# Gate logits folded into the scores and sums products of a pre-norm MoE decoder layer, with routing one period later

## What is computed

```python
# linear attention, 8 heads of 64, elu(.) + 1 as the feature map of q and k
x = x + linear_attention(LN(x))
# cross attention to 77 context rows; scores are normalised per row, then softmax
q = LN(x) @ xWq + xbq; k = ctx @ xWk + xbk; v = ctx @ xWv + xbv
s = q @ k.T / sqrt(512); s = (s - mean(s)) / (std(s, ddof=1) + 1e-8) + mask * -1e-32
x = x + tile(softmax(s) @ v, 16) @ Wout + bout
# mixture of 8 experts, top 2, capacity 1280 rows each, first come first served
h = LN(x); logits = h @ Wg.T; top_v, top_i = top_k(logits, 2); gates = softmax(top_v)
pos = cumsum(one_hot(top_i)) - 1; keep = pos < 1280
x = x + sum over kept choices of gate * ((gelu(h @ W1a) * (h @ W1b)) @ W2)[expert]
```

## Time and profile before

| | |
|---|---|
| runs of the kernel | 1607.64, 1612.87, 1614.09 us; median 1612.87 |
| the profiled execution | 1614.39 us; its span 1612.7 us |
| mean granted clock of TensorE in it | 0.958 of full speed |
| busy: TensorE, VectorE, ScalarE, POOL | 1507.6, 662.7, 542.6, 360.3 us |
| second stage, from 289.6 to 554.0 us | 264.4 us, TensorE busy 236.72, granted clock 0.86 |
| from 554.0 to 591.0 us | 37.0 us, TensorE busy 4.40 |

### The profile page before, as it was taken

The page is one execution under the profiler, slowest core; times in us unless marked ns, Lnnn a source line. Parts: engine busy times, 40 slices in busy tenths (PEclk is TensorE's granted clock), DMA queues, the critical chain, the costliest instruction groups (busy, mean ns, idle before and its releaser), DMA issues.

```text
span 1612.7 us, 21589 instructions
## 1 busy us (share of the span) xinstructions
PE 1507.6 (93%) x7686; PEld 1271.4 (79%) x7687; DVE 662.7 (41%) x1393; ACT 542.6 (34%) x881; POOL 360.3 (22%) x354
## 2 busy tenths in 40 slices
PE   6999999899998549999999989999999999999998
PEld 5778877788876338788888968888978978898886
DVE  6635555576777614331143243114532332214311
ACT  5334333244433414331143243124432332124311
POOL 3213123135543520201211220121121121021011
PEclk9999999998998569999999999999999999999999
DMA  9101222044424431521233252123452162024122
GB/s 190 53 1 52 80 79 105 1 157 132 99 85 131 131 105 54 157 60 31 37 121 91 52 145 70 33 33 117 124 159 46 36 175 46 20 52 130 22 43 26
DMA packets 78987, 132.23 MB, mean 82 GB/s; under 512 B 30388, under 2 KB 30516, under 8 KB 77912
## 3 DMA queue, kind: packets, MB, share of 16 engines
q1 hardware_dynamic: 62520, 97.40, 20.6%
q0 software_dynamic: 16416, 34.16, 11.4%
HBM read 93.63 MB, written 37.91 MB: 82 GB/s over the span
## 4 chain that ended last, share of the span: by engine, by line
PE 82%; DVE 5%; issue 3%; DMA 3%; POOL 3%; ACT 2%; another core or an unknown queue 1%; SPq 0%; ACTq 0%; POOLq 0%; DVEq 0%
PE pg L877 15%; PE pg L878 15%; PE pg L879 15%; PE pj L877 9%; PE pj L879 8%; PE pj L878 8%; PE pj L1079 2%; POOL slot_table L574 2%; PE pg L1048 1%; PE pg L1128 1%; PE pt L1226 1%; DMA stage<-w 1%; DVE w_lo L1289 1%; PE pt L1070 1%
## 5 line engine op out<-in xcount | busy, mean ns | idle before, releaser
L877 PE MATMUL pg<-xe_hi,w_hi 128*128 128x512 f32 (+2 forms) x1088 | 393.9, 362 | 22.4 <-issue 10.6
L878 PE MATMUL pg<-xe_lo,w_hi 128*128 128x512 f32 (+2 forms) x1088 | 393.1, 361 | 0.0
L879 PE MATMUL pg<-xe_hi,w_lo 128*128 128x512 f32 (+2 forms) x1088 | 392.6, 361 | 0.0
L1641 DVE TENSOR_TENSOR hp<-gl,pg 128x512 f32<-128x512 f32 (+1 forms) x136 | 87.1, 641 | 606.1 <-ACT gl L830 596.1
L632 POOL DMA_INDIRECT out_rows<-ost,etab x62 | 100.3, 1618 | 800.0 <-ACT ost L857 396.3
L877 PEld LDWEIGHTS pg<-xe_hi,w_hi 128*128 128x128 f32 x1088 | 207.6, 191 | 54.2 <-issue 12.2
L879 PEld LDWEIGHTS pg<-xe_hi,w_lo 128*128 128x128 f32 x1088 | 207.7, 191 | 28.3
L830 ACT ACTIVATE gl<-pg 128x512 f32<-128x512 f32 (+1 forms) x136 | 76.1, 560 | 457.0 <-PE pg L879 452.7
L878 PEld LDWEIGHTS pg<-xe_lo,w_hi 128*128 128x128 f32 x1088 | 207.5, 191 | 28.3
L877 PE MATMUL pj<-w_hi,hg_hi 128*128 128x512 f32 x464 | 183.4, 395 | 0.0
L879 PE MATMUL pj<-w_hi,hg_lo 128*128 128x512 f32 x464 | 180.8, 390 | 0.0
(11 more groups left out here) (220 smaller groups left out, 2067.6 us busy)
## 6 DMA issues: line engine op xcount, KB each, us to landing
stage<-w SPq DMA_DIRECT2D x96, 512.0 KB, 5.2
xr<-x SPq DMA_DIRECT2D x8, 1024.0 KB, 7.6
out_rows<-xr SPq DMA_DIRECT2D x8, 1024.0 KB, 4.7
x_rows<-xn SPq DMA_DIRECT2D x8, 1024.0 KB
x_in<-x SPq DMA_DIRECT2D x7, 1024.0 KB, 5.2
late_xT<-xT_hi SPq DMA_DIRECT2D x2, 1024.0 KB, 3.9
late_xT<-xT_lo SPq DMA_DIRECT2D x2, 1024.0 KB, 6.0
xT_hi<-late_xT SPq DMA_DIRECT2D x2, 1024.0 KB, 6.1
```

The costliest lines, as they stand in the source:

```text
L877: nc.tensor.matmul(o, lh, rh, start=start, stop=False)
L878: nc.tensor.matmul(o, lh, rl, start=False, stop=False)
L879: return nc.tensor.matmul(o, ll, rh, start=False, stop=stop)
L1641: v.tensor_tensor(hp[j % 2][:, 0:w], gl[j % 2][:, 0:w], pg[:, 2 + j % 2, 0:w], ALU.mult).then_inc(s_hp, 1)
```

## The change

The logits are linear in x2 = x1 + values / sum, so they are split: the x1 part comes with the scores (eight more columns of the 96 in `wqk`, filled with `wgp`), the value part with the sums (`slg`: `emask` and vp times wgp, nine columns instead of one). VectorE adds the two (`logits`). x2 is not turned any more; `xT3`, `turn_and_route` and `logits_out` go. New in the first stage, at `s == 2`: `turn_vp` and `value_logits` on TensorE, `vp_turned_out` and `value_logits_out` on VectorE. Routing stands last in VectorE's period, and positions, slots and `dest` follow in the next. The late jobs move one place. ScalarE's `normalise3` moves from the start of a period to behind `gate_exp`. In the last period POOL's scatter of group 6 is cut in two around `norm3(7)`.

```diff
-LATE_AT = {(-1, 0): [0], (0, 0): [1], (0, 1): [2], (0, 2): [3], (1, 0): [4], (1, 1): [5], (1, 2): [6],
+LATE_AT = {(-1, 0): [0], (-1, 2): [1], (0, 0): [2], (0, 1): [3], (0, 2): [4], (1, 0): [5], (1, 1): [6],
...
@@ SP
-                    if g == 2 * q:
+                    if g == q:
@@ POOL
-                    scatter(g - 2)
-                late_q(late(g, 0))
-                late_q(late(g, 1))
+                    scatter(g - 2, range(TI * TOPK))
+                late_q(late(g - 1, 2))
                 if g + 1 < GROUPS:
                     rstd_1(g + 1)
                 else:
-                    scatter(g - 1)
+                    scatter(g - 1, range(TI * TOPK // 2))
+                late_q(late(g, 0))
                 norm3(g)
                 if g + 1 < GROUPS:
                     sigma(g + 1)
-                late_q(late(g, 2))
+                else:
+                    scatter(g - 1, range(TI * TOPK // 2, TI * TOPK))
+                late_q(late(g, 1))
@@ ScalarE
             for g in range(GROUPS):
-                if g >= 1:
-                    normalise3(g - 1)
...
                 turned(sT[:], 0)
-                late_q(late(g, 0))
+                late_q(late(g - 1, 2))
                 if g >= 1:
                     gate_exp(g - 1)
-                late_q(late(g, 1))
+                    normalise3(g - 1)
                 if g + 1 < GROUPS:
-                    turned_rows(xT2, range(TI), 1)
-                    late_q(late(g, 2))
...
-                turned_rows(xT3, range(TI), 1)
-                if g + 1 < GROUPS:
+                    turned_rows(xT2, range(2), 1)
+                    late_q(late(g, 0))
+                    late_q(late(g, 1))
+                    turned_rows(xT2, range(2, TI), 1)
...
                     score_exp(g + 1)
@@ TensorE
+            def turn_vp():
+
+                pe.wait_ge(s_vpev, 1)
+                for b in range(NB):
+                    for m in range(KC):
+                        ins = nc.tensor.transpose(pt[b][:, m * CK:(m + 1) * CK],
+                                                  vp[:, b * D + m * P:b * D + (m + 1) * P], ident[0:CK, 0:CK])
+                ins.then_inc(s_xset, 1)
+
+            def value_logits():
+
+                pe.wait_ge(s_xev, 3)
+                for b in range(NB):
+                    for m in range(KC):
+                        ins = mm(pt[0][0:CK, b * EX:(b + 1) * EX], vpT[:, b, m * CK:(m + 1) * CK], wgp[:, m, :],
+                                 start=m == 0, stop=m == KC - 1)
...
+            def scores(g, at):
+                if g:
+                    pe.wait_ge(s_sinv, g)
+                if g >= 2:
+                    pe.wait_ge(s_posev, g - 1)
...
-                    ins = mm(pj[0][:, i:i + 1], sT[:, i * P:(i + 1) * P], emask[:, b:b + 1], start=True, stop=True)
+                    ins = mm(pj[0][:, SUMS + i * (1 + EX):SUMS + (i + 1) * (1 + EX)], sT[:, i * P:(i + 1) * P], slg[:, b, :],
+                             start=True, stop=True)
...
-            late_q(late(-1, 0), -1)
             attend(0, range(2))
             keys_values(1)
             attend(0, range(2, TI))
+            late_q(late(-1, 0))
...
+            at_x1 = turn_x1(0, range(TI))
+            scores(0, at_x1)
+            attend(1, range(2))
+            late_q(late(-1, 2))
             for g in range(GROUPS):
                 more_groups = g + 1 < GROUPS
-                if more_groups:
-                    attend(g + 1, range(2))
                 at_e = turn_exp(g)
-                late_q(late(g, 0), g)
-                if g:
-                    positions(g - 1)
                 if more_groups:
                     attend(g + 1, range(2, TI))
-                late_q(late(g, 1), g)
+                if g >= 1:
+                    positions(g - 1)
+                sums(g, at_e)
+                late_q(late(g, 0))
                 if more_groups:
-                    at_x1 = turn_x1(g + 1, range(2), 1)
-                values(g, at_e)
+                    at_x1 = turn_x1(g + 1, range(2))
+                    late_q(late(g, 1))
+                values(g, range(2))
                 if more_groups:
...
+                    at_x1.update(turn_x1(g + 1, range(2, TI)))
+                values(g, range(2, TI))
+                if more_groups:
+                    scores(g + 1, at_x1)
+                    if g + 2 < GROUPS:
+                        attend(g + 2, range(2))
+                    late_q(late(g, 2))
+                else:
+                    positions(g)
@@ VectorE
+                ins = v.tensor_copy(lgx[g % 2][:], pj[0][:, 0:TI * PADW].rearrange("p (i c) -> p i c", c=PADW)
+                                    [:, :, CK:CK + EX])
...
+            def logits(g):
+
+                dve.wait_ge(s_sum, g + 1)
+                both = pj[0][:, SUMS:SUMS + TI * (1 + EX)].rearrange("p (i c) -> p i c", c=1 + EX)
+                v.reciprocal(sinv[:], both[:, :, 0])
+                v.tensor_copy(lgs[:], both[:, :, 1:1 + EX]).then_inc(s_sinv, 1)
+                dve.wait_ge(s_sinv, g + 1)
+                link(v.tensor_tensor(lgs[:], lgs[:], sinv[:].unsqueeze(2).broadcast_to([P, TI, EX]), ALU.mult))
+                v.tensor_tensor(lg[:], lgs[:], lgx[g % 2][:], ALU.add).then_inc(s_lg, 1)
...
             def positions_out(g):
 
                 dve.wait_ge(s_pos, g + 1)
+                if g + 1 < GROUPS:
+                    dve.wait_ge(s_sum, g + 2)
...
             for g in range(GROUPS):
-                if g >= 1:
-                    logits_out(g - 1)
-                    route(g - 1)
...
+                logits(g)
+                if not more_groups:
+                    route(g)
                 cross_out(g)
-                if 1 <= g < GROUPS - 1:
-                    gates(g - 1)
-                    place_tokens(g - 1)
-                if g + 1 < GROUPS:
+                if more_groups:
                     score_stats(g + 1)
+                    if g >= 1:
+                        place_tokens(g - 1)
                     softmax(g + 1)
+                    route(g)
+                gate_diff(g)
```

More of the change, by code:

```diff
@@ L126, in decoder @@
     sinv = keep("sinv", [P, TI])
+    slg = keep("slg", [CK, NB, 1 + EX])
+    lgx = [keep(f"lgx{q}", [P, TI, EX]) for q in range(2)]
+    lgs = keep("lgs", [P, TI, EX])
     lg = keep("lg", [P, TI, EX])
@@ L569, in norm3, with scatter @@
                 p.tensor_tensor(shift[1][:], neg_mean[1][:], rstd[1][:], ALU.mult).then_inc(s_rstd3, 1)
-            def scatter(g):
+            def scatter(g, columns):
                 pool.wait_ge(s_dest, g + 1)
-                for c in range(TI * TOPK):
+                for c in columns:
                     p.indirect_dma_start(
@@ L774, in _ @@
             late_q(late(-1, 0))
[L775 removed]
+            turned_rows(xT2, range(TI), 1)
             def score_exp(g):
@@ L889, in turn @@
                         pe.wait_ge(s_vpev, 1)
+                    if s == 3:
+                        pe.wait_ge(s_xev, 4)
                     if s == NG + 1:
@@ L952, in project @@
                         xattn_values()
+                    if s == 2 and j == TI:
+                        turn_vp()
+                    if s == 2 and j == TI + 1:
+                        value_logits()
                     if s or j >= 2:
@@ L1061, in bank, with turn_x1 @@
                 return pt[k]
[L1063 removed]
+            def turn_x1(g, tiles):
                 at = {}
                 for i in tiles:
[L1066 to L1068 removed]
+                    pe.wait_ge(s_x1, g * TI + i + 1)
+                    to = bank((1 + i) % 2)
                     for k in range(KC):
[L1070 removed]
+                        ins = nc.tensor.transpose(to[:, k * P:(k + 1) * P], xr[g % 4][:, i, k * P:(k + 1) * P],
+                                                  ident[:])
                     ins.then_inc(s_bt, 1)
@@ L1114, in turn_exp, with sums, values @@
                 return nt[0]
-            def values(g, at):
+            def sums(g, at):
                 b = g // NG
                 pe.wait_ge(s_btev, at)
-                if g:
-                    pe.wait_ge(s_posev, g)
                 for i in range(TI):
-                    ins = mm(pj[0][:, i:i + 1], sT[:, i * P:(i + 1) * P], emask[:, b:b + 1], start=True, stop=True)
+                    ins = mm(pj[0][:, SUMS + i * (1 + EX):SUMS + (i + 1) * (1 + EX)], sT[:, i * P:(i + 1) * P], slg[:, b, :],
+                             start=True, stop=True)
                 ins.then_inc(s_sum, 1)
-                for i in range(TI):
+            def values(g, tiles):
+                b = g // NG
+                for i in tiles:
                     if g + 1 < GROUPS and i % 2 == 0:
@@ L1378, in xattn_scores_out, with vp_turned_out, value_logits_out @@
                                   src.rearrange("p (b c) -> p b c", b=NB))
+                for b in range(NB):
+                    v.tensor_copy(wqk[:, :, b * PADW + CK:b * PADW + CK + EX], wgp[:])
```

(17 more changed lines are left out.)

142 lines of the change are left out of this document (48 added, 94 removed).

## The result

| | before | after |
|---|---|---|
| runs of the kernel, us | 1607.64, 1612.87, 1614.09, 1612.79 | 1665.28, 1664.80, 1660.50, 1662.37 |
| median, us | 1612.83 | 1663.59 |
| ratio, 95% interval | | 1.0316 (1.029 to 1.034) |
| span of the profiled execution | 1612.7 | 1663.6 |

The changed kernel is slower by 3.2%, outside the range (1588 to 1628). The stretches of its profile, against those of the earlier trace rows: us, busy PE, PEld, DVE, ACT, POOL, PEclk, DMA share, GB/s. The first seven are the periods between score exponentials, then come the tail to the end of the last scatter, the way to the first expert product, and the expert stage.

The account below looks back on a forecast made before the run. TensorE bounds the periods before; afterwards a chain through TensorE and VectorE. Periods +1.6, tail -3.2, first stage +2.7, opening +0.8 sum to +1.9; with the shown median 1.5 lower than the profiled execution, 1615 us, range 1588 to 1628.

Parts of the forecast that it names:

- Expert stage: The final stage, 1022.13 us of the profile: claimed to be left alone by the change, so 0.
- slower rival: Low clock outlasts the first projection and takes values, turn and scores too: +12 us, 1627; chance 0.25.
- Added work in the first stage: 8 transposes (0.9) and 8 small products (1.8) on TensorE, VectorE's copies hidden beside a projection: +2.7 us.
- The tail: Eighth exponential to last scatter: earlier routing and a split scatter shorten POOL's chain from 45.5 to 42.3 us, -3.2.
- The periods: Seven periods between score exponentials: 186.5 us at full clock plus 30 for clock falls, 216.5 against 214.87, +1.6.
- the walk: Step-by-step timing of one new period: 28.4 us at full clock, bound by a chain through TensorE and VectorE.
- new wait for frl: In a period, TensorE's second projection waits for ScalarE's late copies and reads of the first projection's bank: 1.8 us.
- The clock: TensorE's granted clock falls to half in every period, losing 5 us in each of six: 30 us.
- full-clock rival: TensorE's clock holds in the periods: 1585 us without any fall, 1600 taken with half of them; chance 0.29.
- Late results: Scatter beside a 1 MB store makes ScalarE and VectorE see TensorE's results late; moving normalise3 counted as no gain.

Follow-up runs that it names:

- a_pad32: Changed kernel plus 32 one-element activations on ScalarE ahead of its expert loop: 1630.62 us, ratio 1.0116 to the kernel before.
- p_front: a_pad32 with value_logits one projection later on TensorE and VectorE: 1624.12 us, ratio 1.0059 to the kernel before.
- a_pad20: Changed kernel plus 20 one-element activations on ScalarE ahead of its expert loop: 1630.45 us, ratio 1.0129 to the kernel before.
- a_pad128: Changed kernel plus 128 one-element activations on ScalarE ahead of its expert loop: 1661.95 us, ratio 1.0290 to the kernel before.
- p_fill: a_pad32 plus unused 96-column filler products at the end of TensorE's periods (28 or 60 each): 1648.09 us, ratio 1.0224 to the kernel before.
- v_store: p_front plus two dest and pack buffers, second projection behind values 0 and 1, and normalise3 ending ScalarE's periods except the last: 1608.10 us, ratio 0.9972.
- c_pair: p_front plus two dest and pack buffers, and attention_out's second pair ahead of positions_out on VectorE: 1606.34 us, ratio 0.9954 to the kernel before.

## Why the prediction was wrong

**Expert stage, 0, measured +30.1: the step that decided it.** I wrote that the change "leaves alone" that stage, and took instructions to be free of place. Removing ScalarE's copies of x2 moved its loop, and each of seven jumps back then cost 7.8 to 9.8 us, against 1.0 to 1.9 before. Without that effect the change is +17 us (a_pad32, ratio 1.0116), 2.6 us above the top of the range, and of the sign of the slower rival.

**Added work in the first stage, +2.7, measured +8.7.** 1.6 us of it were there before the second transposes (16.52 against 14.95 us, weights that arrived later; the runs differ by as much). The failed step is "VectorE's six small copies and the wait for s_xev lie beside a projection": the projection was too short a cover, the wait 2.67 us, and the clock fell behind it for 3.4 us, which at half rate loses 1.7. The added products themselves took 0.50 and 1.13 us (1.6, 2.7 forecast). These make 7.6 of the 8.7 us; 1.1 were not traced. p_front takes out 6.5 us of the kernel's time; in its trace the way from the second transposes to the `k_sum` products is 270.45 us, against 276.11 in the changed kernel and 268.99 before.

**The tail, -3.2, measured +3.3.** I counted the landing of each scatter only as POOL's own wait, and took norm3(7) to stand ready. I did not ask what is queued behind VectorE's dest(6). By terms: first scatter 10.7 (9.9 forecast), wait 6.4 (5.6), norm3 late by 3.5 (0), last wait 5.1 (3.5), which is 6.7 of the 6.5 us missed, the halves being slightly shorter.

**The periods, 216.5, measured 222.3: nearly right.** With the same instructions in the periods a_pad20 and a_pad128 took 217.7, nearer still, but the 5 us between them come from which falls an execution gets, and that the walk did not foresee. Periods 2 to 5 sum to 134.2 us against 4 x 33.4 = 133.6. The walk's new wait for frl was 1.9 us in each of five (1.8 forecast), VectorE waits for values as said. TensorE's busy time was 24.5 to 29.4 us (26 to 28 forecast). The walk's 28.4 at full clock is 29.4 where a trace shows it, in a period without a scatter. Two errors lie in it: positions_out was taken as free at t = 6.4, and it ended a wait at 10.8 to 10.9 in every period with a scatter, and the sixth period took 32.8 us, not 28.7, since that late second pair held values for 3.8 us and the clock was at 0.70. In the walk itself 0.3 us of the 28.4 has no term: softmax ends at 28.1.

**The clock.** "I expect a fall in every period" held for six of the seven. Periods 2 to 5 are 4.1 us over the 29.43 on the mean (5 forecast), so the size was fair; the full-clock rival failed. The rule of the Trainium skill by which it would have come (TensorE: Matmul & The Clock Gate, HAM oscillation) explains falls by idle gaps; p_fill, with no gap over 1.3 us for some 10 us ahead of a fall, does not agree with that as the whole cause. What does hold the clock was not settled.

**The slower rival** (the low clock taking in values and scores) is what the sixth period shows, at some 4 us, and not the 12 that I gave it (half of the 2 x 7.9 and 12 that it names would be 14); the result had its sign for other reasons.

**Late results.** "Where the scatter's descriptors and a 1 MB store run together" names the wrong partner: v_store has no such store beside the scatter, and VectorE's wait is the same. The forecast counted no gain and no cost for it; the same lateness then held positions_out, which c_pair shows to be worth 8.0 us.

## What to carry to other kernels

A loop has a place in its engine's program, and any edit ahead of it moves the loop. On ScalarE that alone cost 30 us here: when a stage that was not touched changes its time, look for "issue" waits at the jumps back and at the instruction queues first, and try a few idle instructions. Count the semaphore instructions too. When a step is moved to a later place in a queue, write down for each wait in it what is now queued behind: here what stood behind a dest that waited for a landing, and behind a positions_out that waited for the sums, cost 13 and 8 us, and each went away by a second buffer or by swapping two calls. An edit that takes work off the bounding engine pays only once the waits of the new chain are taken out, which here turned +1.2% into -0.9%.

## What the runs showed of the hardware

- ScalarE's jump back to the head of a loop of 286 instructions (229 without the semaphore ones) cost 7.8 to 9.8 us with the loop at 441 or 569 of its program and under 2.4 us at 461, 473 and 505; the queue that loads it moves 8.2 kB at a time, five packets a round at 441 and 569 and, after the first round, none at the others.
- VectorE's wait on sums of TensorE ended 1.3 to 1.45 us after POOL's last indirect DMA in five periods (for instance 392.69 us, POOL's having ended at 391.32), whether the clock was low or full (sums that ended at 390.72 and at 423.31 were seen at 392.69 and 426.50), and 1.1 to 1.4 us after it in v_store, without the x3 store. In the second period, which has no scatter, it ended with the sums (354.47). In c_pair a wait for attend inside a scatter was not held (380.69, attend having ended at 380.66, POOL's last DMA at 384.04). The mechanism is open.
- TensorE's granted clock fell to half at 424.8 us of p_fill, with no gap over 1.3 us since 407 (granted clock 1.00 through the 6.39 us of 96-column products, then attend and 8-column products with gaps of 1.16 and 1.17 us).
